# Splitting 56 columns between TensorE and the gathers: 25 and 31 where it was 24 and 32, in the last five layers of a graph network

## The reference, cut to what matters

```python
xi, xj = xt[dst], xt[src]
h = einsum(concat([xi, xj, ee]), pW) + pb          # one message per edge
ssum = segment_sum(h, dst); mean = ssum / max(cnt, 1); mx = segment_max(h, dst)
out = einsum(concat([xt, mean, ssum, mx]), poW) + pob
x = relu(out @ lW + lb)                            # five times
x = layernorm(x_in + x)                            # x_in: the rows before the five layers
```

## Time and profile before

| | |
|---|---|
| median of 3 executions | 11153.6 us (11150.61 to 11157.28) |
| span of the profiled execution | 11151.7 us |
| PE busy, share of the span | 10314.4 us, 92% |
| PEld busy | 9851.2 us, 88% |
| DVE, ACT, POOL busy | 8123.2, 6691.2 and 8033.1 us |
| mean granted clock of TensorE | 0.970 |
| the five layers, first pick to last gather | 5114.0 to 11063.0 us |

### The profile page before, as it was taken

How to read it: one execution, slowest core, us unless ns; L and a number is a source line. 1 busy time by engine, 2 the same in 40 slices (tenths; PEclk the granted TensorE clock), 3 DMA queues, 4 the chain that set the end, 5 groups by cost and what they waited for, 6 DMA issues and landing times. The chain is left out here.

```text
span 11151.7 us, 151197 instructions
## 1 busy us (share of the span) xinstructions
PE 10314.4 (92%) x54349; PEld 9851.2 (88%) x54349; DVE 8123.2 (73%) x11930; ACT 6691.2 (60%) x6650; POOL 8033.1 (72%) x8209
## 2 busy tenths in 40 slices
PE   4999579996999999998999899989999899989998
PEld 4999578885999999997999899979999899989997
DVE  4766578886999999996666666666666666666666
ACT  2444245555999999994555455555555455545554
POOL 5777777775766666664777777777777777777776
PEclk8999799997999999999999999999999999999998
DMA  7444154434333333332333333333333333333333
GB/s 239 144 128 126 54 96 99 99 99 128 88 90 89 88 91 88 88 86 74 110 107 110 96 110 110 109 99 104 110 108 105 96 110 110 108 96 110 110 110 92
DMA packets 670413, 1174.96 MB, mean 105 GB/s; under 512 B 198121, under 2 KB 456582, under 8 KB 650550
## 3 DMA queue, kind: packets, MB, share of 16 engines
q1 hardware_dynamic: 366218, 837.19, 22.8%
q0 software_dynamic: 287360, 294.17, 13.1%
q10 hardware_dynamic: 16504, 40.39, 1.2%
HBM read 790.81 MB, written 422.62 MB: 109 GB/s over the span
## 5 line engine op out<-in xcount | busy, mean ns | idle before, releaser
L2512 PE MATMUL ps<-qs,oh 128*128 128x416 f32 (+1 forms) x27200 | 5342.7, 351 | 124.6 <-ACT oh L2598 59.6
L2327 POOL DMA_INDIRECT l3g<-TQ,srcs x4440 | 4262.8, 960 | 1534.8 <-issue 1057.2
L2512 PEld LDWEIGHTS ps<-qs,oh 128*128 128x128 f32 x27200 | 4912.6, 188 | 401.7 <-DVE l3g L2711 210.7
L2711 DVE TENSOR_REDUCE l3g<-ps 128x32 f32<-128x416 f32 x3400 | 1920.1, 584 | 1568.3 <-PE ps L2512 1568.3
L2598 ACT CAST oh<-nd 128x1536 fp32r<-128x1536 bf16 x1140 | 1676.8, 1471 | 1722.5 <-DVE nd L2705 1722.5
L2191 PE MATMUL ps<-l2mm,l2oh 128*128 128x384 f32 (+3 forms) x12544 | 2311.6, 346 | 24.5 <-DVE l2mm L2265 24.5
L2191 PEld LDWEIGHTS ps<-l2mm,l2oh 128*128 128x128 f32 x12544 | 2279.1, 188 | 40.6 <-DVE l2mm L2265 25.3
L2175 POOL DMA_INDIRECT l2g<-Y,place x1568 | 1605.0, 1024 | 738.2 <-issue 396.4
L2265 DVE TENSOR_TENSOR l2mm<-l2hl,psv 128x1664 fp32r<-128x1664 f32 x784 | 1474.0, 1880 | 0.0
L2206 ACT ACTIVATE l2oh<-l2far,l2one 128x512 fp32r<-128x512 f16 x1568 | 1135.8, 724 | 218.3 <-PE ps L2191 45.4
L1601 PE MATMUL ps<-qs,l1oh 128*128 128x442 f32 (+1 forms) x5376 | 1060.5, 357 | 213.2 <-issue 145.6
(11 more groups left out here) (470 smaller groups left out, 7039.9 us busy)
## 6 DMA issues: line engine op xcount, KB each, us to landing
W<-l3o SPq DMA_DIRECT2D x140, 1792.0 KB
mneg<-KG SPq DMA_DIRECT2D x280, 384.0 KB
l3km<-KG SPq DMA_DIRECT2D x280, 360.0 KB
l3g<-TQ,srcs POOLq DMA_INDIRECT x4440
l3t<-AT SPq DMA_DIRECT2D x140, 448.0 KB, 3.9
W<-l1o SPq DMA_DIRECT2D x28, 952.0 KB, 4.1
l0e<-U_a SPq DMA_DIRECT2D x28, 896.0 KB, 4.7
S<-RX SPq DMA_DIRECT2D x49, 512.0 KB
```

The source lines that it names most:

```text
L2327: e.indirect_dma_start(G3[s][:, j, :], None, TQ, bass.IndirectOffsetOnAxis(ap=srcs[:, c * C + j:c * C + j + 1], axis=0)).then_inc(z3[f"g{s ...
L2512: x_ = e.matmul(ps[(KPX * l + k) % 3][:, 0:32 * w], OH[(l + k // SB) % 2][:, g, 128 * (k % SB):128 * (k % SB) + 128], QS[:, p, 32 * n0:32 ...
L2711: e.tensor_reduce(G3[i % 3][:, C - KP + k if k < KP else C - KPE + k - KP, :], ps[r % 3][:, 0:32 * PH].rearrange("p (h f) -> p f h", f=32) ...
```

## The change

TensorE picks 25 columns of each chunk and POOL gathers 31. (The last chunk of a layer keeps 32 and 24.) The blocks of one-hot matrices hold 13 and 12 columns, and in a layer's last chunk 13, 12, 4 and 3, so it has four blocks for three. Buffer 0 of `OH` holds 13 columns, buffer 1 holds 12, and which one a block takes goes by its place in the chunk. Since picks go round three PSUM banks and 25 is no multiple of 3, TensorE's loop holds three chunks, for 9 iterations, with the last chunk behind it. For the larger blocks' room, the second buffers of `KB` and `KM` are put into `X`, which is stored to DRAM at the start of the five layers and read back, into a buffer of `G3`, near their end; the second `OB` goes from `nd2` to `nd`. Because of the latter, DVE waits for the first block to be widened before it makes the first table.

```diff
-KPH = KP // 2
-SB = 12
-NB3 = KP // SB
-SPREAD = ((), (), (0,), (), (1,), (), (2,), (), (3,), (), (), ())
+KP3 = 25
+BLOCKS3 = (13, 12, 4, 3)
+SB = BLOCKS3[0]
+NB3 = 2
+SPREAD = ((), (), (0,), (), (1,), (), (2,), (), (3,), (), (), (), ())
-KPX = 8
-KPE = KP + KPX
+KPX = 7
+KPE = KP3 + KPX
-SPREADX = ((0,), (), (1,), (), (2,), (), (3,), ())
+SPREADX = ((0,), (1,), (2,), (3,), (0,), (1,), (2, 3))
...
+def place3(k):
+    b = sum(1 for x in range(1, len(BLOCKS3)) if k >= sum(BLOCKS3[:x]))
+    return b, k - sum(BLOCKS3[:b])
...
-            KB = [mneg[:, 64 * SB * i:64 * SB * (i + 1)].bitcast(F16) for i in range(2)]
-            KM = [sb(ph, f"l3km{i}", [128, SB * 128], F16) for i in range(2)]
+            KB = [mneg[:, 0:W0_].bitcast(F16), Xf[:, 0:W1_].bitcast(F16)]
+            KM = [sb(ph, "l3km", [128, SB * 128], F16)[:, :], Xf[:, W1_:2 * W1_].bitcast(F16)]
+            XR = G3[(ALL3 - 3) % 3][:, 0:NC, :]
...
-            OB = [nd2f[:, 64 * SB * i:64 * SB * (i + 1)].bitcast(BF16) for i in range(2)]
+            OB = [t_[:, 0:W0_].bitcast(BF16) for t_ in (nd2f, ndf)]
...
             keys(0)
+            e.dma_start(node_view(NH), X[:, :, :]).then_inc(z3["parked"], 16)
+            load(0)
+            e.wait_ge(*z3.at("xc", NGR))
+            e.wait_ge(*z3.at("parked", 16))
             keys(1)
-            load(0)
...
+                if l == 4:
+                    e.wait_ge(*z3.at("add", 2 * (ALL3 - 2)))
+                    e.dma_start(XR, node_view(NH)).then_inc(z3["back"], 16)
                 store(l * NCH + NCH - 1)
...
-                with nc.Fori(0, NCH // 2 - 1, engines=[e.engine], hint_back_edge=True, head_slot={e.engine: 0}) as t:
-                    for d in range(2):
-                        chunk3(l, t, d, KP)
+                with nc.Fori(0, NCH // 3, engines=[e.engine], hint_back_edge=True, head_slot={e.engine: 0}) as t:
+                    for d in range(3):
+                        chunk3(l, t, d, KP3)
                 i = (l + 1) * NCH
-                chunk3(l, None, i - 2, KP)
                 chunk3(l, None, i - 1, KPE)
...
                 for g in range(PG):
                     widen(blocks3(i) + 3, g)
+                for g in range(PG):
+                    widen(blocks3(i) + 4, g)
...
+                    e.wait_ge(*z3.at("back", 16))
-                    a = vc.up(e.tensor_tensor(nd[:, c0:c1, :], XC[:, c0:c1, :], X[:, c0:c1, :],
+                    a = vc.up(e.tensor_tensor(nd[:, c0:c1, :], XC[:, c0:c1, :], XR[:, c0:c1, :],
...
             one_hots(0, range(PG))
+            e.wait_ge(*z3.at("oh", PG))
...
-                        one_hots(blocks3(i) + k // SB + 1, SPREAD[k % SB] if k < KP else SPREADX[k % SB])
+                        b, r = place3(k)
+                        one_hots(blocks3(i) + b + 1, SPREAD[r] if k < KP3 else SPREADX[k - KP3])
```

More of the change, by code:

```diff
@@ L423, in program @@
             QS = sb(ph, "qs", [128, 2, HB * 32], F32R)
[L424 to L425 removed]
+            Xf = X[:, :, :].rearrange("p a b -> p (a b)")
+            W0_, W1_ = (64 * n for n in BLOCKS3[0:2])
+            KB = [mneg[:, 0:W0_].bitcast(F16), Xf[:, 0:W1_].bitcast(F16)]
+            KM = [sb(ph, "l3km", [128, SB * 128], F16)[:, :], Xf[:, W1_:2 * W1_].bitcast(F16)]
+            XR = G3[(ALL3 - 3) % 3][:, 0:NC, :]
             QD = sb(ph, "l3qd", [128, 32])
[L427 to L428 removed]
+            OH = [sb(ph, f"oh{i}", [128, PG, BLOCKS3[i] * 128], F32R) for i in range(2)]
+            OB = [t_[:, 0:W0_].bitcast(BF16) for t_ in (nd2f, ndf)]
             ETf = ET[:, :, :].rearrange("p a b -> p (a b)")
@@ L473, in program @@
         z3 = Named(sem, "l3", "g0 g1 g2 e ob oh red qd add scan lay o0 o1 kb0 kb1 tq out qn parts pk mm eev mr z zt zts "
-                              "nmm masks xc xt xts pq rep wide four xa ap wr px",
+                              "nmm masks xc xt xts pq rep wide four xa ap wr px parked back",
                    z1.over(g0=16 * (C - KP) * 14, g1=16 * (C - KP) * 14, starts=16 * NC, root=2 * NGR, tab=2, hat=NGR,
@@ L479, in program @@
                            kb1=KD4 * NB1 * NCH // 2, ob=PG * NB1 * NCH, oh=PG * NB1 * NCH, qd=17, pk=KP * NCH,
-                           red=RED0 + KP * NCH, parts=3, ma=1, mea=1, fixed=1))
+                           red=RED0 + KP * NCH, parts=3, ma=1, mea=1, fixed=1) + kg.over(cell=16, placed=CQ))
         def meet(e, k):
@@ L2349, in keys @@
                 i, b = block3(m)
-                n = SB if b < NB3 else KPX
-                key_block(e, KB[m % 2][:, 0:128 * n], KM[m % 2][:, 0:128 * n],
-                          KQ * (i % NCH) + (KQ - KP + SB * b if b < NB3 else KQ - KPE), n, z3[f"kb{m % 2}"])
+                n, k = BLOCKS3[b], sum(BLOCKS3[:b])
+                key_block(e, KB[b % 2][:, 0:128 * n], KM[b % 2][:, 0:128 * n],
+                          KQ * (i % NCH) + (KQ - KP3 + k if k < KP3 else KQ - KPE + k - KP3), n, z3[f"kb{m % 2}"])
             def load(i):
@@ L2492, in at @@
                 def at(each, more):
-                    return more + each * d if t is None else t * (2 * each) + (more + each * (l * NCH + d))
+                    return more + each * d if t is None else t * (3 * each) + (more + each * (l * NCH + d))
                 def mix(s):
@@ L2511, in chunk3 @@
                             n0, w = PICKS[g]
-                            x_ = e.matmul(ps[(KPX * l + k) % 3][:, 0:32 * w],
-                                          OH[(l + k // SB) % 2][:, g, 128 * (k % SB):128 * (k % SB) + 128],
+                            x_ = e.matmul(ps[(picked3(l * NCH) + KP3 * (d % NCH) + k) % 3][:, 0:32 * w],
+                                          OH[b % 2][:, g, 128 * r:128 * r + 128],
                                           QS[:, p, 32 * n0:32 * (n0 + w)],
@@ L2595, in widen @@
                     h, d = block3(m - 1)
-                    e.wait_ge(*z3.at("pk", picked3(h) + SB * d))
-                w = 128 * (SB if b < NB3 else KPX)
-                e.copy(OH[m % 2][:, g, 0:w], OB[g % 2][:, 0:w]).then_inc(z3["oh"], 1)
+                    e.wait_ge(*z3.at("pk", picked3(h) + sum(BLOCKS3[:d])))
+                w = 128 * BLOCKS3[b]
+                e.copy(OH[b % 2][:, g, 0:w], OB[g % 2][:, 0:w]).then_inc(z3["oh"], 1)
             for g in range(PG):
```

26 lines of the change are left out of this document (14 added, 12 removed).

## The result

The changed kernel takes **11178.42 us** (median of 16 runs, 11174.11 to 11187.02), the kernel before beside it 11153.97 (16 runs, 11150.36 to 11164.63): ratio 1.0021, 95% interval [1.0015, 1.0028]. The prediction had 11162, a range of 11090 to 11225, and for the forecast itself 11145 to 11178. So the sign and the place near "no change" came out; the loss is 24 us where 8 were forecast. It lies 2 us above 11176, which the prediction called the upper bound of "same", a hair over the forecast's own 11145 to 11178, and well within the whole range.

What follows compares the result with a forecast made beforehand. Gathers were taken to bind most chunks by 0.95 us over TensorE's 39.48. Later chunks -4.9, first chunks +3.8, layer ends +2.6 and +6.0, start +0.5 gave +8: 11162 us by the median, range 11090 to 11225.

Steps and rivals of the forecast that it cites:

- What binds before: In most chunks of the five layers, 32 gathers on POOL (40.43 us) bind by 0.95 over TensorE's 39.48.
- Stall (a): TensorE waits at the chunk's end for ACT's widening of the next chunk's last group; 0.70 us a chunk, to go.
- Stall (b): TensorE waits in a chunk's first 17 picks for reduces delayed by DVE's scans; 0.65 us a chunk, to stay.
- A chunk is 40.24: Later chunks in the changed kernel: 39.48 + 1.46 for the added pick - 0.70 for the boundary stall = 40.24 us.
- 24 picks are 35.04: TensorE's picks in a chunk of the kernel before, at 1.46 us each, total 35.04 of its 39.48 us.
- First chunks +3.8: Each layer's first chunk gets a pick and loses the boundary stall: +0.76 us five times, +3.8.
- Layer ends: Last chunks: 2.0 us stall before pick 29, net +0.5 each, +2.6 in all; transitions to the next layer 1.5 each, +6.0.
- The loop of three: TensorE's loop body grows from 824 to 1284 instructions; taken as 0, or 0 to 5.8 us a turn if fetched.
- X: Its store to DRAM and read back near the layers' end are hidden; without cover each costs 6 us once.
- (a) stays: Slower rival: the last widening is late, so the chunk-end stall remains; up to 95 us, 11257; chance 0.05.
- (b) goes: Faster rival: DVE clears its backlog, so the scan stall vanishes; chunk 39.6, 83 us less, 11079; chance 0.12.
- (b) grows: Slower rival: TensorE without its boundary rest keeps DVE busier; 0.2 to 0.5 us a chunk, up to 11227; chance 0.13.

Runs made afterwards that it cites:

- e1: The kernel before with one gather less in every chunk and no pick more: 11049.89 us, ratio 0.9905 to the kernel before.
- e3: The changed kernel with the mixes after picks 17, 19, 21 and 23 instead of 16, 18, 20 and 22: 11266.33 us, ratio 1.0101 to the kernel before.
- e4: The changed kernel with additions after picks 1 and 2, scans after 3, 6, 9, 12 (were 2, 4; 6, 8, 10, 12): 11093.79 us, ratio 0.9946 to before.
- e2: The changed kernel with one more gather per chunk, into a spare tile that moves the one-hot tiles 384 bytes: 11160.92 us, ratio 1.0006 to the kernel before.
- e7: The changed kernel with nine chunks in TensorE's loop instead of three: 13703.88 us on a slow chip, ratio 0.9827 to the kernel before there.
- e8: The kernel before with only X stored to DRAM and read back as in the change: 13922.3 us on a slow chip, ratio 0.9997 to the kernel before there.

## Why the prediction was nearly right

**What binds before** (gathers, by 0.95 us, in 110 of 130 chunks): right. e1 took the bound away, and the chunks became 39.49.

**Gathers and VectorE's idle time go**: right, 188.2 us in 120 places to none.

**Stall (a), 0.70, goes**: right in place, size and reason. The gap is gone in after: by the starts of the picks 0.60 at the boundary and 0.09 of restart. e3 puts it back, at 0.70 of chunk.

**Stall (b), 0.65, stays**: right, and it grew by 0.04. e4 removes it, and the chunk falls by 0.65. The prediction's floor without it was 39.6; it is 39.68.

**A chunk is 40.24**: 0.09 short, and this term made most of the miss: 130 x 0.09 = 11.8 of the 15 us. By the starts of the picks, a chunk of before that gathers don't hold (39.48) and one of after (40.33):

| part of the chunk | before | after | difference | forecast |
|---|---|---|---|---|
| boundary, last pick to the next chunk's first, with the added pick | 2.26 | 3.12 | +0.86 | +0.86 |
| first pick behind the boundary | 1.56 | 1.47 | -0.09 | -0.10 |
| the next ten picks, undisturbed | 14.61 | 14.67 | +0.05 | 0 |
| four picks at the scans, stall (b) | 6.46 | 6.50 | +0.04 | 0 |
| eight picks with the mixes | 14.59 | 14.58 | -0.01 | 0 |
| sum (rounded apart) | 39.48 | 40.33 | +0.85 | +0.76 |

The term that was mis-sized is "24 picks are 35.04", taken over from before unchanged. In before most chunks have their first picks 1.460 apart; in after, where TensorE doesn't stop at the boundary, all have 1.467, and ten such picks are 0.05. The other half, 0.04, is stall (b), which the prediction called unchanged. The stop that went had a faster rhythm behind it. That the faster rhythm comes only behind a stop is what e1, e3, e4 and the two kernels show; why, they don't.

**First chunks +3.8**: measured +9.8. The pick and stall (a) account for 3.8; the other 6 are the clock at 1.2 GHz over the first picks, in five layers of after and two of before. It isn't shown to be the change's work: e1, without it, has one such layer; with it e4 has three (the third, fourth and fifth), e3 one and a first layer at 0.74, e2 five. The forecast had no term for it. What decides it at a layer's start is open.

**Layer ends**: the stall ahead of pick 29 was 1.45 of idle time, 1.7 by the distance of the picks, for 2.0. The chunk's +0.5 held all the same, in part by luck: its other parts came 0.2 longer than forecast. A transition, with two groups to compare behind the last pick, cost 1.0 more, not 1.5.

**The loop of three** costs nothing: right. q8 is silent, all 135 boundaries have 1.47 us from pick to pick, and e7 shows what a fetched turn would look like. Of the Trainium skill's two statements in "Runtime: NRT & Kernel Launch" ("Instruction fetch mechanics"), the one on a window of two pages would have every loop here fetch; q8 shows that of the longest alone. The one on 2048 instructions agrees with all three: 824 and 1284 kept, 3852 fetched on each turn.

**X**: right, 0.9997 [0.9981, 1.0013] in e8, with the reservation on the slow comparisons.

**The rivals.** "(a) stays" would have been 0.70 a chunk, as e3 shows, and +88 us, near the 95 given. "(b) goes" did not happen by itself; done by hand it gave 11094, near the 11079 given. "(b) grows" came true in small: by 0.04 a chunk, 5 us, where 0.2 to 0.5 was given.

## What to carry to other kernels

Before an engine is given more work, list its stalls one by one with what ends each: here a pick of 1.46 us was paid for with one stall of 0.70 and a bound of 0.95 that held only in most chunks, and the sum was known beforehand to be about nil. Then ask for the stall that is left; the 0.65 behind four scans in a row was worth 85 us, more than three times what the whole change moved, for an edit of a few lines. And where a forecast is the difference of two large sums, look at what holds a rhythm as well as at its size: here the picks ran 0.5% faster only behind the very stop that the change took away. Say beforehand how much a hundredth of a microsecond in a chunk is; here it is 1.3 us.

## What the hardware showed unexpectedly

- **The rhythm of the same matmuls depends on where their tiles lie.** Eight matmuls of 384 or 416 columns with their loads take 1.453 us in the six traces that have 384 bytes ahead of the one-hot tiles, and 1.460 or 1.467 in the eight that don't. The six are from four chips. Which property of the address does it, the runs don't tell.
- **It depends on a stop as well.** With tiles in one place, first picks at 1.460 stand in 31 of 125 chunks where TensorE stops at the chunk's boundary (e3), and in none where it doesn't (after, e4).
- **TensorE's clock at a layer's start varies between executions of like kernels**: a granted 0.50 or 1.00 over the first 3 us (once 0.74), at 0.50 in one to five layers of five, for some 1.9 us each. In e4 the layers that began at the full clock lost 1.4 of it again, waiting for a gather.
- **On three chips every kernel ran about a quarter longer** (the kernel before 13913 to 14169 us for 11154) with VectorE's and POOL's operations of the same length, and one kernel's ratio to another moved from 0.972 to 1.013 between two of them. A narrow interval within one comparison says nothing of that. Whether the chips or the time of the runs made it is open: all eight came after the four others.
- **A loop body of 3852 instructions is fetched on every turn** (287 packets for 61) and costs an estimated 0.5 us at the turn (1.96 to 2.03 us from pick to pick for 1.47); one of 1284 isn't, and costs nothing.
